# Token buffers that take six loads early, and the context expert splits moved on VectorE

## What is computed

```python
x = x + xattn(layernorm(x), ids, ctx, ctx, ctx)   # y = (silu(h @ ctx[e].T) * (h @ ctx[e].T)) @ ctx[e].T
x = x + ffn(layernorm(x), ...)                    # e = min(id // 6250, 3), one of 4 experts by token id

def ffn(hidden):                                  # 2048 tokens, H = 512, I = 256, E = 32, K = 4
    h = rmsnorm(hidden, norm_w)
    scores = softmax(h @ gate_w.T); w, ids = top_k(scores, 4)
    routed = sum over the 4 chosen experts of w * (silu(g) * u) @ w2[e],  g, u = split(h @ w13[e])
    shared = silu(h @ shared_gate) * (h @ shared_up) @ shared_down
    return hidden + routed + shared
```

## Time and profile before

| | us |
|---|---|
| median of 3 runs | 655.73 |
| lowest and highest | 654.82, 656.04 |
| the profiled execution | 656.32 |
| its span, first to last instruction | 654.6 |
| PE busy | 620.7 (95%) |
| DVE busy | 441.6 (67%) |
| ACT busy | 364.1 (56%) |
| POOL busy | 351.3 (54%) |

### The profile page before, as it was taken

How to read it: one execution, slowest core, us unless ns; L and a number is a source line. 1 busy time by engine, 2 the same in 40 slices (tenths; PEclk the granted TensorE clock), 3 DMA queues, 4 the chain that set the end, 5 groups by cost and what they waited for, 6 DMA issues and landing times.

```text
span 654.6 us, 15525 instructions
## 1 busy us (share of the span) xinstructions
PE 620.7 (95%) x3246; PEld 506.3 (77%) x3247; DVE 441.6 (67%) x1044; ACT 364.1 (56%) x635; POOL 351.3 (54%) x366
## 2 busy tenths in 40 slices
PE   2799999999999999999999999999999999999993
PEld 1678788887788887888888888888888888888882
DVE  6778888876899995655765566755665666656520
ACT  5456666655443214466665666756656656656531
POOL 3735777646511115436747656456565576466623
PEclk9999999999999999999999999999999999999997
DMA  7321223437976627767998999999988999899545
GB/s 279 120 106 61 109 99 124 156 150 234 364 174 143 124 38 135 235 176 182 292 289 212 231 255 247 265 248 244 214 207 216 282 258 239 234 222 233 100 57 68
DMA packets 45007, 124.70 MB, mean 191 GB/s; under 512 B 5808, under 2 KB 6960, under 8 KB 44464
## 3 DMA queue, kind: packets, MB, share of 16 engines
q0 software_dynamic: 24256, 59.26, 41.1%
q1 hardware_dynamic: 20720, 65.09, 30.2%
HBM read 90.51 MB, written 39.06 MB: 198 GB/s over the span
## 4 chain that ended last, share of the span: by engine, by line
PE 71%; DMA 2%; POOL 1%; issue 1%; ACT 0%; SPq 0%; POOLq 0%; ACTq 0%
PE sps_gu L229 14%; PE sps_gu L231 14%; PE sps_gu L230 13%; PE sps_t L231 6%; PE sps_t L230 6%; PE sps_t L229 6%; PE sps_rank L1043 3%; PE sps_table L1043 3%; PE sps_cols L1043 3%; PE sps_table L1106 2%; PE sps_y L229 1%; PE sps_y L230 1%; PE sps_y L231 1%; DMA both<-hb_dram 1%; DMA hb_dram<-craw,sidx 1%; DMA both<-hb_dram,gather 1%
## 5 line engine op out<-in xcount | busy, mean ns | idle before, releaser
L1495 DVE TENSOR_TENSOR wl<-raw,wh x87 | 105.4, 1224 | 48.1 <-ACT wh L1263 45.2
L229 PE MATMUL sps_gu<-wh,s_xth 128*128 x320 | 133.0, 416 | 0.0
L231 PE MATMUL sps_gu<-wh,s_xtl 128*128 x320 | 126.2, 394 | 0.0
L1017 POOL DMA_INDIRECT both<-hb_dram,e_gidx x76 | 90.4, 1189 | 64.3 <-DVE e_gidx L1455 47.2
L230 PE MATMUL sps_gu<-wl,s_xth 128*128 x320 | 124.9, 390 | 0.0
L1263 ACT ACTIVATE wh<-raw x87 | 90.6, 1059 | 10.1 <-issue 9.8
L1031 POOL DMA_INDIRECT out<-r_oh,e_sidx x40 | 65.7, 1644 | 48.3 <-issue 14.4
L1234 ACT ACTIVATE both<-sps_gu 128x256 f32<-128x256 f32 x80 | 30.8, 385 | 90.5 <-PE sps_gu L231 90.5
L231 PEld LDWEIGHTS sps_gu<-wh,s_xtl 128*128 128x128 f32 x320 | 60.0, 188 | 14.3
L1462 DVE TENSOR_TENSOR both<-both,sps_gu 128x256 f32<-128x256 f32 x80 | 33.4, 418 | 54.4 <-ACT both L1234 54.4
L229 PE MATMUL sps_t<-wh,s_ath 128*128 x160 | 69.2, 433 | 0.1
(11 more groups left out here) (348 smaller groups left out, 1435.7 us busy)
## 6 DMA issues: line engine op xcount, KB each, us to landing
raw<-in_experts_w SPq DMA_DIRECT2D x96, 512.0 KB, 5.3
craw<-in_ctx_w SPq DMA_DIRECT2D x4, 1024.0 KB, 7.9
both<-hb_dram SPq DMA_DIRECT2D x16, 256.0 KB, 4.5
out<-hb_dram SPq DMA_DIRECT2D x4, 1024.0 KB, 15.2
out<-both POOLq DMA_DIRECT2D x13, 256.0 KB, 4.0
both<-hb_dram,e_gidx POOLq DMA_INDIRECT x76, 6.0
out<-r_oh,e_sidx POOLq DMA_INDIRECT x40, 6.1
sraw<-in_sg SPq DMA_DIRECT2D x1, 512.0 KB, 5.4
```

The source lines that it names most:

```text
L229: pe.matmul(acc, left_hi, right_hi, start=start, stop=False)
L231: return pe.matmul(acc, left_lo, right_hi, start=False, stop=stop)
L1017: pool.indirect_dma_start(e_xg[:, t.ring], None, hn_rows, bass.IndirectOffsetOnAxis(ap=gidx[:, t.ring:t.ring + 1], axis=0)).then_inc(e_gx[ ...
L1495: dve.tensor_tensor(m.wl[:, w, ROWS[part], :], m.raw[:, bass.ds(x % 2, 1), ROWS[part], :], m.wh[:, w, ROWS[part], :].bitcast(F32), ALU.sub ...
```

## The change

In the context stage:
- The split of expert 0 becomes two halves of 128x1024. The first is made in step 2 and counted in a new semaphore `ctx_first`, the second in step 3 (`ctx_split`). PE's first product of tile 0 waits for `ctx_first` alone, and for `ctx_split` before its second half.
- The splits of experts 1, 2 and 3 stand in DVE's part `front` of steps 5, 6 and 7, where they stood in steps 3, 4 and 5.
- ACT's `h` of tile 1 is emitted ahead of the high half of tile 0 in step 3, where it came last of the two and `keep`.

In the shared stage the token tiles 8 to 13 get six buffers of their own, over memory of the context stage that is free once its last `x1` is done. Their loads wait for no turn; load 8 waits for all `x1`. Tiles 14 and 15 take the first two buffers of the ring and wait for the turns of tiles 4 and 5.

```diff
-            def product(dst, hi, lo, t):
+            def product(dst, hi, lo, t, first=False):
                 e = bass.ds(expert[t.off], 1)
                 for c in range(C):
+                    if first and c == C // 2:
+                        pe.wait_ge(m.s["ctx_split"], 1)
...
                 elif part == "g1":
-                    pe.wait_ge(m.s["ctx_split"], expert[t.off] + 1)
+                    first = isinstance(t.n, int) and t.n == 0
+                    if first:
+                        pe.wait_ge(m.s["ctx_first"], 1)
+                    else:
+                        pe.wait_ge(m.s["ctx_split"], expert[t.off] + 1)
...
-                elif part == "h":
+                elif part == "h" and isinstance(t.n, int) and t.n == 1:
+                    return
+                elif part == "early" and not (isinstance(t.n, int) and t.n == 1):
+                    return
+                elif part in ("h", "early"):
...
-            pipeline(act, pairs, [("base", 9), ("x2", 8), ("t1hi", 3), ("keep", 2), ("weights", 0), ("h", 2), ("silu", 4), ("t2hi", 5)], emit)
+            pipeline(act, pairs, [("base", 9), ("x2", 8), ("early", 2), ("t1hi", 3), ("keep", 2), ("weights", 0), ("h", 2), ("silu", 4), ("t2hi", 5)], emit)
...
+            def first_low(half):
+                part = slice(half * C // 2, (half + 1) * C // 2)
+                return dve.tensor_tensor(m.ctl[:, 0, part], craw[:, 0, part], m.cth[:, 0, part].bitcast(F32), ALU.subtract)
...
                     if t.n == 2:
                         front_stats(2)
-                        low(0)
+                        dve.wait_ge(m.s["ctx_hi"], 1)
+                        first_low(0).then_inc(m.s["ctx_first"], 1)
                     elif t.n == 3:
-                        low(1)
+                        first_low(1).then_inc(m.s["ctx_split"], 1)
                     elif t.n == 4:
                         front_stats(3)
-                        low(2)
+                    elif 5 <= t.n < 4 + E1:
+                        low(t.n - 4)
                 elif part == "weights":
                     if isinstance(t.n, int):
-                        if t.n == 5:
-                            low(3)
...
+        SPARE = 6
+        with ExitStack() as lent:
+            spare_tiles = m.sb("spare_tiles", [P, SPARE, D], F32, lent)
...
+        def place(i):
+
+            if 2 * RING <= i < 2 * RING + SPARE:
+                return spare_tiles[:, i - 2 * RING], s[f"lent{i - 2 * RING}"], 16
+            n = i if i < 2 * RING else i - SPARE
+            return xg[:, n % RING], gx[n % RING], 16 * (n // RING + 1)
+
+        def before(i):
+
+            return i - RING if i < 2 * RING else i - RING - SPARE
...
-                wait(sp, s["t1"], i - RING + 1)
-                sp.dma_start(xg[:, i % RING], m.hb_dram[i * P:(i + 1) * P, 0:D]).then_inc(gx[i % RING], 16)
+                if i == 2 * RING:
+                    sp.wait_ge(m.c["x1"], 2 * pairs)
+                if not 2 * RING <= i < 2 * RING + SPARE:
+                    sp.wait_ge(s["t1"], before(i) + 1)
+                tile, landed, _ = place(i)
+                sp.dma_start(tile, m.hb_dram[i * P:(i + 1) * P, 0:D]).then_inc(landed, 16)
...
-                    pe.wait_ge(gx[i % RING], 16 * (i // RING + 1))
+                    tile, landed, count = place(i)
+                    pe.wait_ge(landed, count)
                     wait(pe, s["t1lo"], i - RING + 1)
-                    turn(turned[i % RING], xg[:, i % RING], C).then_inc(s["t1"], 1)
+                    turn(turned[i % RING], tile, C).then_inc(s["t1"], 1)
```

More of the change, by code:

```diff
@@ L244, in build @@
         m.s = {n: top.enter_context(nc.semaphore(n)) for n in (
-            "consts", "chain0", "chain1", "ctx_hi", "ctx_split", "gate_hi", "gate_split", "counted",
+            "consts", "chain0", "chain1", "ctx_hi", "ctx_split", "ctx_first", "gate_hi", "gate_split", "counted",
             "onehot", "table", "tid_loaded", "norm_loaded", "gate_loaded", "sh_loaded", "sh_hi", "prefix", "zero_pad",
@@ L547, in emit @@
                 elif part == "g1":
-                    pe.wait_ge(m.s["ctx_split"], expert[t.off] + 1)
+                    first = isinstance(t.n, int) and t.n == 0
[3 more added lines that the diff above has]
+                        pe.wait_ge(m.s["ctx_split"], expert[t.off] + 1)
                     pe.wait_ge(s["t1lo"], t.n + 1)
                     wait(pe, s["a"], t.n - 1)
-                    product(ps_z[t.par], hth, htl, t).then_inc(s["g1"], 1)
+                    product(ps_z[t.par], hth, htl, t, first).then_inc(s["g1"], 1)
                 elif part == "t2":
@@ L819, in shared_routing_and_experts @@
             "base", "t1", "t1hi", "t1lo", "logits", "lrow", "back", "shifted", "exp", "top",
-            "marked", "counted", "ranked", "g1", "sil", "a", "t2", "t2hi", "t2lo", "g2", "y", "sum0", "sum1", "sum2", "sum3", "sum4", "chain", "pchain",
+            "marked", "counted", "ranked", "g1", "sil", "a", "t2", "t2hi", "t2lo", "g2", "y", "sum0", "sum1", "sum2", "sum3", "sum4", "chain", "lent0", "lent1", "lent2", "lent3", "lent4", "lent5", "pchain",
             "tile_col", "tile_row", "hot", "table", "slots", "last_row", "raw0_a", "raw0_b", "raw0_c", "raw1_a", "raw1_b", "raw1_c", "w_hi", "w_lo"))
```

## The result

The changed kernel takes 662.85 us (median of 5 runs, 661.76 to 664.56), the kernel before 654.82 us (5 runs, 654.53 to 656.04). The ratio is 1.0118, interval 1.0100 to 1.0135: slower, by about 8 us. The forecast was 661.8 us, range 658.5 to 666.0. The profiled execution took 662.85 us with a span of 661.1 us, 6.5 us more than the span before. That is less than 8 because the profiled execution before, 656.32 us, was a long one for that kernel.

The account below looks back on a forecast made before the run. PE was taken to bound the kernel (71% of the span). Front +5.5, clock +2.0 and buffers -1.4 on the profiled 656.32 us gave 662.4; with the median 0.59 lower, forecast 661.8 us, range 658.5 to 666.0.

Parts of the forecast that it names:

- Tiles 0 to 2: Context front: turn of tile 1 near 23.18, 0.75 us won; PE about 1.4 us ahead by the turn of tile 2.
- The step that decides: Products of tiles 1 and 2: splits now behind `a` on DVE leave PE idle 3.85 and about 4.8 us; front net +5.5.
- The clock: After PE's two new gaps: clock halves, 2.0 us per fall; one fall likeliest, +2.0 us, chance 0.45.
- the rival with two falls: Both PE gaps in the context front bring a clock fall; total 663.8 us, chance 0.25.
- Nothing later gives it back: Context stage after the front: the +5.5 us stays, as PE has next to no idle time until 140 us.
- Buffers: Between context and shared stage: earlier loads 8 to 11 let the last store take 3.5 us, not 5.27; -1.4 us.
- The sum: Whole kernel: +5.5 + 2.0 - 1.4 on the profiled 656.32 us gives 662.4; forecast median 661.8 us.

Follow-up runs that it names:

- warm_second: Changed kernel with 64 small unread matmuls on PE ahead of the wait for the split of expert 2 only; 661.45 us, ratio 1.0099.
- front_only: Kernel before with all the change's context-stage edits and none of its shared-stage edits; 664.92 us, ratio 1.0148.
- half_guarded: Changed kernel with one added DVE wait: first half split of expert 0 starts only after POOL has tile 1's bias; 662.36 us, ratio 1.0110.
- placed_spread: `splits_placed` with the three pieces of the shared expert's split in DVE steps 8, 10 and 11 instead of 8, 9 and 10; 653.28 us, ratio 0.9962.
- splits_early: Changed kernel with split 1 ahead of step 4's statistics, split 2 ahead of `a` in step 5, split 3 at step 6's end; 655.09 us, ratio 0.9997.
- buffers_only: Kernel before with the change's shared-stage token buffers alone, context front as before; 654.02 us, ratio 0.9982.
- buffers_held: `buffers_only` with loads 8 to 11 waiting for the turns of tiles 4 to 7 again; 654.83 us, ratio 1.0001.
- splits_placed: Changed kernel with splits 1 and 2 early, split 3 in DVE's step 6 idle time, splits waiting for POOL's bias; 652.48 us, ratio 0.9958.
- split1_early: Changed kernel with only the split of expert 1 moved, to DVE's step 4 ahead of tile 3's statistics and tile 0's `a`; 659.81 us, ratio 1.0066.

## Why the prediction was right, point by point

- **Tiles 0 to 2.** The turn of tile 1 was forecast at 23.18 and stood at 23.59 in an execution that started 0.47 us late: right to 0.1 us. The turn of tile 2 was to end at 27.1, it ended at 27.41, 26.94 without the late start. But this first gain is not certain; it rests on the split starting after POOL's last step for tile 1, which in the trace of before it did by a hair (20.93 in both). I read the two equal times and did not see that they could swap. Where they swap, 0.85 to 1.04 us of it is lost (`warm_second` and `front_only`, counted from the first warming batch). Nor did I see that the second warming batch can last longer: 2.44 us in `half_guarded`, 2.73 in `placed_spread`, and then it holds the turn.
- **The step that decides.** Forecast 3.85 and 4.8 us of idle time before the products of tiles 1 and 2; measured 3.86 and 4.92. The chain of DVE rows was the right reading, and `splits_early` shows by removal that the order was the cause: the change's loss disappears with it. Without the clock the front costs 9.39 us less the 4.24 us of the two slow products against 2.84 each, that is 5.2 us, where 5.5 was forecast.
- **The clock.** This term was mis-sized. One fall at 2.0 us was taken as likeliest; both gaps brought a fall, at 2.3 and 1.9 us in the profiled execution. The term measured 4.2 us where 2.0 was forecast, and the rival with two falls described what happened. The error was to lean on the single fall at the end of the kernel and to give the shorter gap less weight, though at 3.85 us it was well past those 2.9. Behind the second warming batch the profiles have eight idle stretches of 3.86 to 5.93 us, and each brought a fall, in five cases during the stretch and in three within 0.35 us after PE had resumed. The price was argued from the two warming batches, 2.74 and 1.65 us, and this step is not confirmed: the granted clock reads 1.00 through both, and also in the 4.86 us of idle time ahead of the first.
- **"Nothing later gives it back."** Wrong by 1.2 us. PE was 9.9 us late at the turn of tile 4, 9.8 at that of tile 5 and 8.7 from that of tile 9 on. The trace of before had 0.28, 0.60 and 0.31 us of idle time at tiles 8 to 10, hidden in the 1.29 us by which the earlier trace rows falls short of 95; the changed kernel has 0.45 and 0.23 us at tiles 9 and 10. That is half a microsecond of the 1.2, and that DVE and ACT caught up while PE was late is argued, not tested. The row showed the amount; I called it next to nothing.
- **Buffers.** Forecast -1.4 us, measured 1.2 us alone (`buffers_only`); in the changed kernel PE's wait for tiles 12 and 13 went from 1.47 to 0.22. That the early issue is the cause is shown by `buffers_held`; that it acts by less company for the last store fits the profiles and is not shown apart. The 3.5 us of an undisturbed store was too low a bound to take: it took 3.89 and 4.57.
- **The sum.** 5.5 + 2.0 - 1.4 = 6.1 was forecast. By the rows it was 5.2 + 4.2 for the front, -1.2 in the steps behind it, -1.8 from PE's start of the shared stage to the shared expert's first product (8.70 to 6.93 us late, of which 1.46 are waits for loads), 0.5 for the later start, and about -0.4 in the expert stage, which I did not trace: 6.5, the difference of the spans. The second fall (+2.2) and the returns that were not counted nearly cancel in it.
- **Luck.** The medians differ by 8.0 us, not by 6.5, so the forecast growth of 6.1 was 1.9 us too small. In the time only 1.0 of it shows, because I started from 655.73 us, the median of three runs, and that of five is 654.82. The other difference, 6.5 against 8.0, is the long profiled execution before. A part of its length lies in the front: from the first warming batch to the turn of tile 4 it has 22.5 us, `buffers_only` and `buffers_held` with the same front 21.6 and 21.9, with 0.43 and 0.36 us of idle time before tile 3 instead of 1.25. The changed kernel has 31.9, so its front costs 9.4 to 10.2 us, which agrees with the 9.7 of `front_only`. The forecast was right in mechanism and in the waits, and better in the total than its parts deserve.

The Trainium skill (SBUF — State Buffer, "Who interferes with whom") was used in the prediction for the splits that hold up POOL. The rows agree: POOL's 0.27 us step took 1.32, 2.23 and 2.38 us beside splits of 1.19, 2.28 and 2.31 us. The same section infers that this form of DVE instruction does not delay the writing of DMA descriptors. Here the gather in the earlier trace rows took 2.80 us where a later one in the same trace took 1.04, and it ended 0.93 us behind the split, so a gather issued by POOL is held. Whether it is the writing of descriptors or another part of the gather's work that waits, no run here tells.

## What to carry to other kernels

A step moved in a software pipeline takes on every wait that stands ahead of it in its engine's order: ask not when the engine has idle time, but behind which wait that idle time lies. Here a 2.3 us split was put behind `a`, which waits for the product of one tile, while PE's product of the next tile waits for the split: DVE and PE took turns where they had overlapped. A good place is one where the engine is about to wait anyway (`splits_placed`), and out of the way of small GpSimd steps on which another engine's work hangs.

An idle stretch of TensorE of some microseconds should be priced twice, once for its length and once for the half-speed work behind it; a few matmuls that nobody reads are a cheap way to see which part is which.

## What the runs showed of the hardware that I had not expected

- A VectorE subtraction with both inputs in SBUF and a small GpSimd instruction on 128x1 numbers that start in the same instant: the small one waits for the end of the large one, 2.38 us for work of 0.27. It was held where the subtraction began before it or at most 0.02 us after it (`split1_early`, 25.02 against 25.00), and not where it began 0.2 us after it (`splits_early`, 21.36 against 21.16). So a few tenths of a microsecond in when a gather lands decide it, and they differ between executions.
- The third fall in `front_only` above: PE's wait was of 1.32 us only, between logit products with 32 columns of weights, and in the kernel before a wait of 1.16 us at the same place brought none. So the length of an idle stretch alone does not tell whether the clock falls.
- The clock's fall came 2.0 and 2.2 us after TensorE's last matmul in the front of the changed kernel, 2.9 us after it at the end of the kernel before, and 4.2 and 5.1 us after it in `front_only` (end of the last matmul 27.94, fall 32.1; 37.27 and 42.4), there after TensorE had resumed. The same idle time of 3.86 us cost between 1.6 and 2.4 us in the product behind it. What sets these times stays open.
- The second warming batch, 24 matmuls, took between 1.51 us (`splits_placed`) and 2.73 us (`placed_spread`), with a granted clock of 1.00 in the rows of both. The granted clock alone does not tell how fast these matmuls run.
